# Expert rows that carry their gates, expert outputs stored gated, and early sums behind GpSimd's last store

## The chip, the core and the metric

The kernel runs on one core of a Trainium2 chip: TensorE (PE, with its weight load PEld), VectorE (DVE), ScalarE (ACT), GpSimd (POOL) and SyncE (SP), which work side by side and wait for each other by semaphores, and 16 DMA engines. The metric is device time in microseconds, the median of several runs. All data are float32 (some products are made from a high and a low part).

## The reference, cut to what matters

```
x = x + attn_a(_layernorm(x))      # 8 rows of 512 tokens, 128 wide; 16 heads, softmax
x = x + ffn(_layernorm(x))         # mixture of experts
x = x + attn_b(_layernorm(x))      # linear attention (8 heads) and an MLP
x = x + ffn(_layernorm(x))         # the same mixture of experts again

# ffn, E = 8 experts, K = 2 per token:
probs = softmax(xn @ Wr + br);  scores, idx = top_k(probs, K)
full  = relu(xn @ W1_e + b1_e) @ W2_e + b2_e            # for each expert
c = relu(b1) @ W2 + b2;  c_total = c.sum(axis=0)
output = sum_k scores[k] * (full[idx_k] - c[idx_k] + c_total)
return residual + output
```

So a token's result is a sum of two expert outputs, each plus a constant of its expert and times its gate (the score).

## The kernel before, in words

It runs in three stages: attention (and the first routing), linear attention, MLP (and the second routing). "Row" is one of 8 batch rows of 512 tokens, held as NT = 4 tiles of 128 tokens; with NT tiles per row, x_sb holds the residual.

**Routing** (class Route, `bankR` its PSUM bank). For each row VectorE normalises the tokens into `xn_sb` (profile name f_xn; it is refilled row by row, a ring of 2 or 3), TensorE turns them and makes the logits, ScalarE the exponentials; VectorE takes the two largest (`dve_top`, `dve_topid`), ids and gates (`dve_ids`), and works out in which slot of its expert's region each token's row goes (`dve_place` to `dve_slots`, profile name f_slot). GpSimd then scatters 8 times 128 rows to DRAM (`expert_in`), an indirect DMA each (L703). A row is 130 floats: 128 of the token, the token's number, and the lower one of its two expert ids. `dve_gates` (L679 to L688) puts the two gates in the order of the expert ids into `gates`: six small instructions a row. In the MLP stage the order on VectorE is x_add of the row before, its statistics, two products, then `route_place` with the gates, then the normalisation (L406); on GpSimd a power of the statistics (L367) comes before the eight scatters of the row before, in two halves.

**Experts** (class Experts). Behind each routing, blocks of 256 rows are worked off expert by expert in a loop on all engines. SP loads a block into `xb`; TensorE turns it; VectorE makes `xbT` (L1126); TensorE 8 matmuls up (L1090), ScalarE 4 relus (L1111), TensorE 16 matmuls down (L1100) in two tiles t of 128 tokens. VectorE takes out token number and lower id (`meta`, L1122), works out whether the token's other expert comes first (`second`, L1132) and so the row of `expert_out` to write to (`this_to`, L1137). For each tile it waits until that tile's store of the block before has landed, casts the row numbers (L1143) and adds the expert's constant (L1146, `yb`); GpSimd stores the tile by an indirect DMA (L1158). The order on VectorE within a block: second, this_to, meta and xbT of the next block, cast and y of tile 0, cast and y of tile 1. The first half of `expert_out` has the outputs of each token's lower expert id ("early"), the other half those of its higher one ("late").

**Combine.** SP loads the early rows 0 to 3 (0 and 1 in the first routing) once all experts but the last have stored, the others when the last store has landed. VectorE adds for each tile early output times gate (L758) and late output times gate (L767) to x_sb. In the MLP stage ScalarE's queue then stores each row to the output; in linear attention the rows 2 to 7 are added between other work, two rows ahead.

Of the kernel before, what the change touches and what calls it, by code (L numbers as in the profile page):

```python
# [38 lines left out]
W = D + 2  # L39
# [4 lines left out]
def build_hybrid(nc, x, W_K, W_Q, W_V, W_O, attn_norm_w, Wq, Wk, Wv, Wo, out_norm_w, mlp_norm_w,  # L44
                 Wgate, Wup, Wdown, gamma, beta, Wr, br, W1, b1, W2, b2, out):
    root = ExitStack()
    with root:
# [52 lines left out]
        spare = sb("spare", [1, 16])  # L100
        gates = sb("gates", [P, (B + 1) * NT, TOP])
# [46 lines left out]
        class Startup:  # L148


            CONSTS = 21
            BANKS = (4, 5, 6, 7, 2, 3, 2, 3)

            def __init__(self, at, raw):
# [4 lines left out]
                self.small, self.fill = sem("s_small", at), sem("s_fill", at)  # L159
# [23 lines left out]
            def pool(self, pool):  # L183
                nc.gpsimd.memset(self.zero, 0.0).then_inc(self.fill, 1)
                nc.gpsimd.memset(before_bf[:, :], 0.0).then_inc(self.fill, 1)
                pool.wait_ge(self.fill, 2)
# [23 lines left out]
                nc.gpsimd.memset(gates[:, B * NT:, :], 0.0).then_inc(self.const, 1)  # L210
                nc.gpsimd.memset(fill[:, :, 0:D], 0.0).then_inc(self.const, 1)
                nc.gpsimd.memset(fill[:, :, D + 1], -1.0).then_inc(self.const, 1)
                nc.gpsimd.iota(fill[:, :, D], pattern=[[P, BT]], base=(TOP - 1) * B * T, channel_multiplier=1,
# [276 lines left out]
        class Route:  # L490
# [10 lines left out]
            def __init__(self, name, at, bankR, ring=2, lean=False):  # L501
# [9 lines left out]
                self.topidf = sb(name + "_topidf", [P, NT, E], f32, at=at)  # L511
# [5 lines left out]
                self.gate = sb(name + "_gate", [P, NT, TOP], at=at)  # L517
                self.below = sb(name + "_below", [P, TOP, NT, 1], at=at)
                self.kept_gate = sb(name + "_kept_gate", [P, NT, TOP], at=at)
                self.turned_gate = sb(name + "_turned_gate", [P, NT, TOP], at=at)  # L520
                self.gate_step = sem(name + "_gate_step", at)
# [80 lines left out]
            def dve_ids(self, dve, b, u):  # L602

                self.settle(dve, b, self.TOPID)
                nc.vector.tensor_copy(self.topidf[:, :, :], self.topid[:, :, :]).then_inc(self.step, 1)
                nc.vector.tensor_tensor(self.gate[:, :, :], self.top[:, :, 0:TOP],
                                        self.rrec[:, :, :].to_broadcast([P, NT, TOP]), ALU.mult).then_inc(self.step, 1)

            def dve_is_k(self, dve, b, u):
                self.settle(dve, b, self.IDS)  # L610

                nc.vector.tensor_copy(self.norm.xn_sb[:, u, :, D], token[:, bass.ds(b * NT, NT)]
                                      ).then_inc(self.tagged, 1)
                nc.vector.tensor_tensor(self.norm.xn_sb[:, u, :, D + 1], self.topidf[:, :, 0], self.topidf[:, :, 1],
                                        ALU.min).then_inc(self.tagged, 1)
                for k in range(TOP):
                    nc.vector.tensor_tensor(self.is_k[:, k, :, :],
                                            expert_id[:, :].unsqueeze(1).to_broadcast(self.wide),
                                            self.topidf[:, :, k:k + 1].to_broadcast(self.wide),
# [56 lines left out]
            def dve_gates(self, dve, b, u):  # L676

                first, second = self.topidf[:, :, 0:1], self.topidf[:, :, 1:2]
                nc.vector.tensor_tensor(self.below[:, 0, :, :], first, second, ALU.is_lt).then_inc(self.gate_step, 1)  # L679
                nc.vector.tensor_tensor(self.below[:, 1, :, :], first, second, ALU.is_gt).then_inc(self.gate_step, 1)  # L680
                dve.wait_ge(self.gate_step, 6 * b + 2)
                for k, part in enumerate((self.kept_gate, self.turned_gate)):
                    nc.vector.tensor_tensor(part[:, :, :], self.gate[:, :, :],
                                            self.below[:, k, :, :].to_broadcast([P, NT, TOP]),
                                            ALU.mult).then_inc(self.gate_step, 1)
# [483 lines left out]
        with stage(clear=False) as st:  # L1169
# [69 lines left out]
            with nc.Block(no_gpsimd_drain=True) as block:  # L1239
# [263 lines left out]
                def _(dve):  # L1503
# [121 lines left out]
                    for b in range(2):  # L1625
                        combine.dve_early(dve, b)
# [675 lines left out]
```

## Time and profile before

| | us |
|---|---|
| median of 3 runs (lowest to highest) | 1335.34 (1331.35 to 1336.68) |
| the profiled execution: its own time / its span | 1336.18 / 1333.9 |
| busy PE / DVE / ACT / POOL | 1201.3 / 923.5 / 829.8 / 507.8 |
| POOL's stores of expert outputs, 142 | 139.4 |
| POOL's scatters of tokens, 128 | 126.5 |

The span is the time between the first and the last instruction of the profiled execution. The page cuts it into 40 slices of 33 us; by its rows attention lasts to about 520 us, the first expert blocks from 565 to 697, linear attention from 700 to 1018, the MLP to 1140, its last scatters to 1162, the second expert blocks from 1168 to 1308, and the tail to the end. Busy shares don't say what a change is worth: in each stage another engine has no gap, and an engine's idle time costs only where something else waits for it.

### The profile page before, as it was taken

The numbers are of one execution on the slowest core, as the hardware profiler recorded it, in microseconds if no ns is written. First come the engines' busy times: TensorE is split into PE (matmuls) and PEld (weight loads), VectorE is DVE, ScalarE is ACT, GpSimd is POOL, SyncE is SP. The second block draws the span as 40 slices with busy tenths as digits, with TensorE's granted clock in tenths as the row PEclk, the third lists the DMA queues.
The fourth block names the chain that finished last, engine by engine and source line by source line (L and its number), as shares of the span: only waits on it lengthen the run. The fifth ranks groups of instructions, "written<-read, shape, count | busy, mean of one in ns | idle before, by whom it ended". The sixth has DMA issues, their size and how long they took to land. (4 is left out here: it accounts for less than half of the span.)

```text
span 1333.9 us, 26704 instructions
## 1 busy us (share of the span) xinstructions
PE 1201.3 (90%) x7787; PEld 913.0 (68%) x7787; DVE 923.5 (69%) x3634; ACT 829.8 (62%) x2478; POOL 507.8 (38%) x619
## 2 busy tenths in 40 slices
PE   6999999999999998699975999999996988199991
PEld 4666676666666665499964777777774656189991
DVE  6788888888888875444446888888873676344446
ACT  5898888888989885244432565565555666044440
POOL 2111334142414232545442343443432366635452
PEclk9999999999999999799997999999997999599996
DMA  9100000000000000222222000000000011222226
GB/s 291 53 2 1 12 7 11 7 13 6 17 5 13 7 11 3 77 72 72 69 78 72 9 9 9 9 1 1 1 1 1 13 39 39 74 61 71 70 74 203
DMA packets 54443, 52.90 MB, mean 40 GB/s; under 512 B 7341, under 2 KB 43098, under 8 KB 54330
## 3 DMA queue, kind: packets, MB, share of 16 engines
q1 hardware_dynamic: 36320, 29.39, 7.7%
q0 software_dynamic: 8928, 17.84, 4.0%
q10 hardware_dynamic: 9082, 4.33, 1.1%
q8 instruction: 51, 0.84, 0.3%
q14 instruction: 62, 0.51, 0.1%
HBM read 29.48 MB, written 22.05 MB: 39 GB/s over the span
## 5 line engine op out<-in xcount | busy, mean ns | idle before, releaser
L1462 ACT ACTIVATE prob<-prob,negmax 128x256 f32<-128x256 f32 (+3 forms) x512 | 283.2, 556 | 37.5 <-DVE negmax L1556 37.4
L1556 DVE CUSTOM_DVE_ANT_0 prob<-bank,mask 128x256 f32<-128x256 f32 (+3 forms) x512 | 224.6, 481 | 32.9 <-PE bank L1272 31.2
L1640 POOL TENSOR_TENSOR Vs<-Vh_sb,rinv 128x512 f32<-128x512 f32 x64 | 66.7, 1042 | 355.9 <-DVE rinv L1534 355.9
L1158 POOL DMA_INDIRECT expert_out<-f_x_yb,f_x_to x142 | 139.4, 981 | 155.3 <-DVE f_x_yb L1146 130.8
L1284 PE MATMUL bank<-prob,Vs 128*64 128x512 f32 (+3 forms) x1024 | 153.6, 442 | 2.9 <-POOL Vs L1640 2.8
L703 POOL DMA_INDIRECT expert_in<-f_xn,f_slot x128 | 126.5, 988 | 48.9 <-issue 30.9
L1090 PE MATMUL bank<-f_x_xbT,W_sb 128*128 128x256 f32 x568 | 138.1, 387 | 1.5 <-DVE f_x_xbT L1126 1.5
L1111 ACT ACTIVATE f_x_hid<-bank,cols 128x256 f32<-128x256 f32 x144 | 63.8, 474 | 91.7 <-PE bank L1090 91.7
L1090 PEld LDWEIGHTS bank<-f_x_xbT,W_sb 128*128 128x128 f32 x568 | 104.6, 194 | 14.5 <-DVE f_x_xbT L1126 2.5
L1284 PEld LDWEIGHTS bank<-prob,Vs 128*64 128x64 f32 x1024 | 64.1, 137 | 72.8 <-issue 62.9
L1111 ACT ACTIVATE prob<-bank,cols 128x256 f32<-128x256 f32 x140 | 62.1, 474 | 82.1 <-PE bank L1090 82.1
L1143 DVE CAST f_x_to<-f_x_this_to 128x1 int32<-128x1 f32 x142 | 21.3, 150 | 116.1 <-DMA expert_out<-f_x_yb,f_x_to 115.9
L1462 ACT ACTIVATION_READ_ACCUMULATOR prob<-prob,negmax 128x1 f32 x512 | 97.6, 191 | 0.0
L1851 ACT ACTIVATE yT_hi<-bank 128x512 fp32r<-128x512 f32 x64 | 38.3, 598 | 90.1 <-PE bank L1778 90.1
L1983 DVE SCALAR_TENSOR_TENSOR z_sb<-bank,ro,z_sb 128x128 f32<-128x128 f32 x256 | 88.3, 345 | 6.4 <-POOL ro L1917 2.9
L1272 PE MATMUL bank<-Q_hi,K_hi 64*128 64x256 f32 (+3 forms) x512 | 89.5, 345 | 2.3 <-DVE K_lo L1524 2.3
L1272 PE MATMUL bank<-Q_lo,K_hi 64*128 64x256 f32 (+3 forms) x512 | 83.2, 320 | 0.0
L1272 PE MATMUL bank<-Q_hi,K_lo 64*128 64x256 f32 (+3 forms) x512 | 82.7, 319 | 0.0
L1858 ACT ACTIVATE junk<-bank 128x128 f32<-128x128 f32 x256 | 68.7, 274 | 16.8 <-PE bank L460 4.8
L1272 PEld LDWEIGHTS bank<-Q_hi,K_hi 64*128 64x128 f32 x512 | 48.6, 186 | 42.9 <-issue 39.8
L458 PE MATMUL bank<-WVO_hi,yT_hi 128*128 128x256 f32 x256 | 74.5, 291 | 2.4 <-DVE z_sb L1983 2.4
L460 PE MATMUL bank<-WVO_hi,yT_lo 128*128 128x256 f32 x256 | 72.2, 282 | 0.0
(270 smaller groups left out, 3186.6 us busy)
## 6 DMA issues: line engine op xcount, KB each, us to landing
f_x_xb<-expert_in SPq DMA_DIRECT2D x73, 130.0 KB, 2.2
z_sb<-expert_out SPq DMA_DIRECT2D x20, 256.0 KB, 3.6
expert_out<-f_x_yb,f_x_to POOLq DMA_INDIRECT x142
expert_in<-fill ACTq DMA_DIRECT2D x16, 130.0 KB, 3.0
x_sb<-in_L_attn_a_x_dram SPq DMA_DIRECT2D x8, 256.0 KB, 6.3
W_sb<-in_L_ffn_W_dram SPq DMA_DIRECT2D x1, 2048.0 KB, 9.9
expert_in<-f_xn,f_slot POOLq DMA_INDIRECT x128, 2.4
act_h<-expert_out SPq DMA_DIRECT2D x8, 256.0 KB, 5.7
```

The lines of the kernel that those rows point to most:

```text
L458: nc.tensor.matmul(ps, lhsT_hi, rhs_hi, start=True, stop=False)
L460: return nc.tensor.matmul(ps, lhsT_lo, rhs_hi, start=False, stop=stop)
L703: pool.indirect_dma_start(xg, bass.IndirectOffsetOnAxis(ap=self.slot[:, u, t, k:k + 1], axis=0), self.norm.xn_sb[:, u, t, :], None).then_i ...
L1090: nc.tensor.matmul(self.bankH[c][:, 0:BLK], W1_sb[:, e, c * P:(c + 1) * P], self.xbT[:, :], start=True, stop=True).then_inc(self.up_done[c ...
L1111: nc.scalar.activation(self.hid[:, c, :], self.bankH[c][:, 0:BLK], ACT.Relu, bias=b1_col[:, e * FC + c:e * FC + c + 1]).then_inc(self.hid_ ...
L1158: pool.indirect_dma_start(yg, bass.IndirectOffsetOnAxis(ap=self.to[:, t:t + 1], axis=0), self.yb[:, t, :], None).then_inc(self.stored[t], 16)
L1272: mm = nc.tensor.matmul(score_bank(i, a), left[r, g % 2, tile], right[r, g % 2, 0:width[i]], start=(right is Q_hi and left is K_hi), stop= ...
L1284: mm = nc.tensor.matmul(bankZ[heads, 0:width[i]], Vs[:, g % 2, i, heads], prob[:, g % 2, a, columns(i)], start=(i == 3), stop=(i == 2), sk ...
L1462: nc.scalar.activation(mine, mine, ACT.Exp, scale=-1.0, bias=negmax[:, g % 2, i, a:a + 1], accum_out=rowsum[:, g % 2, i, a:a + 1]).then_in ...
L1556: nc.vector.tensor_tensor_reduce(out=prob[:, g % 2, a, columns(i)], in0=score_bank(i, a), in1=mask[:, T - width[i]:], scale=-1.0, scalar=H ...
L1858: ins = nc.scalar.activation(junk[:, s % 2, m, :], bankO[s % 2 * 2 + m // 2][:, m % 2 * (DB + D):m % 2 * (DB + D) + DB], ACT.Square, accum ...
L1983: nc.vector.scalar_tensor_tensor(out=tile, in0=bankO[s % 2 * 2 + m // 2][:, o:o + D], scalar=ro[:, s % 2, m:m + 1], in1=tile, op0=ALU.mult ...
```

## The change

1. A scattered row grows from 130 to 134 floats: token, two gates, token number, lower id, two ids. The cast of ids and the multiplication that makes the gates write straight into `xn_sb`. `dve_gates`, `gates` and their six instructions a row are gone.
2. In the expert loop VectorE copies the six tags of a row and works out for each token the gate of this expert and the row to write to: three instructions into `part` and `meta`, and one sum `gate_to`. ScalarE multiplies the expert's constant by the gate, two activations a block behind the relus (`gated_const`). y is now PSUM times gate plus `gated_const`, one scalar_tensor_tensor a tile.
3. The sums of Combine are plain: one tensor_tensor of 128x512 for each row in place of four scalar_tensor_tensor.
4. GpSimd does a small memset behind its last store is issued (`all_issued`), and VectorE waits for it before the first early sums, in both routings.

```diff
-W = D + 2
+GATE, TOKEN, LOW_ID, IDS = D, D + TOP, D + TOP + 1, D + TOP + 2
+W = IDS + TOP
@@ Route
-                nc.vector.tensor_copy(self.topidf[:, :, :], self.topid[:, :, :]).then_inc(self.step, 1)
-                nc.vector.tensor_tensor(self.gate[:, :, :], self.top[:, :, 0:TOP],
+                tags = self.norm.xn_sb[:, u, :, :]
+                nc.vector.tensor_copy(tags[:, :, IDS:IDS + TOP], self.topid[:, :, 0:TOP]).then_inc(self.step, 1)
+                nc.vector.tensor_tensor(tags[:, :, GATE:GATE + TOP], self.top[:, :, 0:TOP],
                                         self.rrec[:, :, :].to_broadcast([P, NT, TOP]), ALU.mult).then_inc(self.step, 1)
-            def dve_gates(self, dve, b, u):
...
@@ Combine
-                for t in range(NT):
-                    tile = x_sb[:, b * NT + t, :]
-                    nc.vector.scalar_tensor_tensor(
-                        out=tile, in0=self.early[:, b * NT + t, :], scalar=gates[:, b * NT + t, 0:1],
-                        in1=tile, op0=ALU.mult, op1=ALU.add).then_inc(self.early_added, 1)
+                row = x_sb[:, b * NT:(b + 1) * NT, :]
+                nc.vector.tensor_tensor(row, row, self.early[:, b * NT:(b + 1) * NT, :],
+                                        ALU.add).then_inc(self.early_added, 1)
@@ Experts.act_work
+                    act.wait_ge(self.gate_to_ready, k + 1)
+                    for t in range(BT):
+                        act.wait_ge(self.y_ready[t], k)
+                        ins = nc.scalar.activation(self.gated_const[:, t, :], moe_const[:, e, :], ACT.Copy,
+                                                   scale=self.gate_to[:, t, 0:1])
+                    ins.then_inc(self.const_ready, 1)
@@ Experts.dve_work
-                    nc.vector.tensor_copy(self.meta[:, :, :], self.xb[:, :, D:D + 2]).then_inc(self.meta_ready, 1)
+                    nc.vector.tensor_copy(self.meta[:, :, :], self.xb[:, :, D:]).then_inc(self.meta_ready, 1)
...
+                    gate, low_id, first_id = self.meta[:, :, 0:TOP], self.meta[:, :, LOW_ID - D], self.meta[:, :, IDS - D]
+                    nc.vector.tensor_scalar(self.part[:, :, 1], low_id, float(e), float(B * T),
+                                            ALU.not_equal, ALU.mult)
+                    nc.vector.scalar_tensor_tensor(out=self.part[:, :, 0], in0=first_id, scalar=float(e),
+                                                   in1=gate[:, :, 0], op0=ALU.is_equal,
+                                                   op1=ALU.mult)
+                    nc.vector.scalar_tensor_tensor(out=gate[:, :, 1], in0=first_id, scalar=float(e),
+                                                   in1=gate[:, :, 1], op0=ALU.not_equal,
+                                                   op1=ALU.mult).then_inc(self.parts_known, 1)
...
+                        if t == 0:
+                            dve.wait_ge(self.const_ready, k + 1)
                         dve.wait_ge(self.down_done[t], k + 1)
-                        nc.vector.tensor_tensor(self.yb[:, t, :], self.bankY[t][:, 0:D],
-                                                moe_const[:, e, :], ALU.add).then_inc(self.y_ready[t], 1)
+                        nc.vector.scalar_tensor_tensor(
+                            out=self.yb[:, t, :], in0=self.bankY[t][:, 0:D], scalar=self.gate_to[:, t, 0:1],
+                            in1=self.gated_const[:, t, :], op0=ALU.mult, op1=ALU.add).then_inc(self.y_ready[t], 1)
@@ Experts.pool_work, behind the loop
+                nc.gpsimd.memset(spare[:, 16:17], 0.0).then_inc(self.all_issued, 1)
@@ both routings
                     experts.dve_work(dve, counts)
+                    dve.wait_ge(experts.all_issued, 1)
```

On VectorE in the MLP stage, before, between the slots of one row and the normalised tokens of the next:

```order
L666 TENSOR_REDUCE f_slotf<-f_picked 128x8
L674 CAST f_slot<-f_slotf 128x8
L679 TENSOR_TENSOR f_below<-f_topidf 128x4
L680 TENSOR_TENSOR f_below<-f_topidf 128x4
L683 TENSOR_TENSOR f_kept_gate<-f_gate,f_below 128x8
L683 TENSOR_TENSOR f_turned_gate<-f_gate,f_below 128x8
L688 TENSOR_TENSOR gates<-f_kept_gate,f_turned_gate 128x4 x2
L406 TENSOR_SCALAR f_xn<-x_sb,f_mv,f_power 128x128 x4
```

and at the same place now:

```order
L655 CAST run_bf<-f_run 128x8
L659 TENSOR_REDUCE f_slotf<-f_picked 128x8
L667 CAST f_slot<-f_slotf 128x8
L405 TENSOR_SCALAR f_xn<-x_sb,f_mv,f_power 128x128 x4
L373 TENSOR_SCALAR f_power<-f_power 128x4
```

The six instructions of the gates are gone, and f_xn follows f_slot.

On VectorE in the last expert's blocks, a turn of the loop before:

```order
L1132 TENSOR_SCALAR f_x_second<-f_x_meta 128x2
L1137 TENSOR_TENSOR f_x_this_to<-f_x_second,f_x_meta 128x2
L1120 REGISTER_ALU
L1122 COPY f_x_meta<-f_x_xb 128x4
L1125 REGISTER_ALU
L1126 TENSOR_SCALAR f_x_xbT<-bank,cols 128x256
L1142 REGISTER_ALU
L1143 CAST f_x_to<-f_x_this_to 128x1
L1146 TENSOR_TENSOR f_x_yb<-bank,moe_const 128x128
L1143 CAST f_x_to<-f_x_this_to 128x1
L1146 TENSOR_TENSOR f_x_yb<-bank,moe_const 128x128
```

and now:

```order
L1116 TENSOR_SCALAR f_x_part<-f_x_meta 128x2
L1118 SCALAR_TENSOR_TENSOR f_x_part<-f_x_meta 128x2
L1121 SCALAR_TENSOR_TENSOR f_x_meta<-f_x_meta 128x2
L1127 TENSOR_TENSOR f_x_gate_to<-f_x_part,f_x_meta 128x4
L1103 REGISTER_ALU
L1105 COPY f_x_meta<-f_x_xb 128x12
L1108 REGISTER_ALU
L1109 TENSOR_SCALAR f_x_xbT<-bank,cols 128x256
L1132 REGISTER_ALU
L1133 CAST f_x_to<-f_x_gate_to 128x1
L1138 SCALAR_TENSOR_TENSOR f_x_yb<-bank,f_x_gate_to,f_x_gated_const 128x128
```

Two more small instructions stand ahead of meta and xbT, and y has another form; the rest of the turn is in the same order.

## Rows read from the trace of the kernel before

**Rows 1.** The page's 40 slices, TensorE's busy tenths.

```profile
PE   6999999999999998699975999999996988199991
```

**Rows 2.** Order in time, VectorE, MLP stage: start us, busy us, instruction, [idle before <-releaser].

```profile
1111.60 0.17 DVE L674 CAST f_slot<-f_slotf 128x8 int32<-128x8 f32 x1
...
1112.38 1.31 DVE L406 TENSOR_SCALAR f_xn<-x_sb,f_mv,f_power 128x128 f32<-128x128 f32 x4
```

**Rows 3.** Order in time, MLP stage, ScalarE and TensorE, one row earlier.

```profile
1095.49 1.26 ACT L2133 ACTIVATE m_xn<-z_sb,mlp_rstd 128x128 f32<-128x128 f32 x4
...
1099.48 0.66 PE L431 MATMUL bank<-ident,f_xn 128*128 128x128 f32 x4 [1.30 <-DVE f_xn L406]
```

**Rows 4.** Order in time, GpSimd, MLP stage.

```profile
1109.85 1.67 POOL L367 TENSOR_TENSOR f_power<-f_power,half 128x8 f32<-128x8 f32 x1
1112.63 1.03 POOL L703 DMA_INDIRECT expert_in<-f_xn,f_slot  x1 [1.11 <-DVE f_slot L674]
...
1124.20 1.67 POOL L367 TENSOR_TENSOR f_power<-f_power,half 128x8 f32<-128x8 f32 x1
...
1140.11 1.67 POOL L367 TENSOR_TENSOR f_power<-f_power,half 128x8 f32<-128x8 f32 x1 [2.12 <-DVE f_power L362]
```

**Rows 5.** Order in time, second expert stage, all engines, one turn of the loop.

```profile
1204.95 1.89 PE L1090 MATMUL bank<-f_x_xbT,W_sb 128*128 128x256 f32 x8
...
1205.58 1.77 ACT L1111 ACTIVATE f_x_hid<-bank,cols 128x256 f32<-128x256 f32 x4 [1.97 <-PE bank L1090]
1206.29 0.15 DVE L1143 CAST f_x_to<-f_x_this_to 128x1 int32<-128x1 f32 x1 [1.75 <-DMA expert_out<-f_x_yb,f_x_to]
1206.36 0.28 DVE L1146 TENSOR_TENSOR f_x_yb<-bank,moe_const 128x128 f32<-128x128 f32 x1
...
1207.43 0.54 DVE L1126 TENSOR_SCALAR f_x_xbT<-bank,cols 128x256 f32<-128x256 f32 x1
1207.46 0.96 POOL L1158 DMA_INDIRECT expert_out<-f_x_yb,f_x_to  x1 [1.14 <-DVE f_x_yb L1146]
1207.54 0.37 SPq L1049 DMA_DIRECT2D f_x_xb<-expert_in  x1
...
1207.99 0.29 DVE L1146 TENSOR_TENSOR f_x_yb<-bank,moe_const 128x128 f32<-128x128 f32 x1
...
1208.68 1.89 PE L1090 MATMUL bank<-f_x_xbT,W_sb 128*128 128x256 f32 x8
...
1209.94 0.15 DVE L1143 CAST f_x_to<-f_x_this_to 128x1 int32<-128x1 f32 x1 [1.66 <-DMA expert_out<-f_x_yb,f_x_to]
```

**Rows 6.** Waits of VectorE, second expert stage: us in total, times, longest.

```profile
DVE f_x_to L1143 <- DMA expert_out<-f_x_yb,f_x_to: 57.9, 37, 2.4
```

**Rows 7.** Order in time, VectorE and GpSimd, the tail.

```profile
1308.18 4.28 DVE L758 SCALAR_TENSOR_TENSOR x_sb<-z_sb,gates,x_sb 128x128 f32<-128x128 f32 x16
1308.83 1.06 POOL L1158 DMA_INDIRECT expert_out<-f_x_yb,f_x_to  x1 [2.46 <-DVE f_x_yb L1146]
1310.19 3.11 POOL L1158 DMA_INDIRECT expert_out<-f_x_yb,f_x_to  x1 [0.30 <-issue]
...
1317.36 4.29 DVE L758 SCALAR_TENSOR_TENSOR x_sb<-z_sb,gates,x_sb 128x128 f32<-128x128 f32 x16 [4.90 <-DMA z_sb<-expert_out]
1321.57 8.49 DVE L767 SCALAR_TENSOR_TENSOR x_sb<-act_h,gates,x_sb 128x128 f32<-128x128 f32 x32
```

**Rows 8.** Busy time by stretch: second expert stage, tail (PEclk, DMA share, GB/s last).

```profile
1169.00:1307.00 138.00, 136.70 (x936) 126.43 (x936) 61.92 (x285) 63.82 (x144) 67.20 (x70) 0.99 0.26 76
...
1316.00:1332.50 16.50, 0.00 (x0) 0.00 (x0) 12.70 (x48) 0.00 (x0) 0.00 (x0) 0.50 0.97 314
```

**Rows 9.** The page's costliest groups: xcount | busy us, mean ns | idle before.

```profile
L1983 DVE SCALAR_TENSOR_TENSOR z_sb<-bank,ro,z_sb 128x128 f32<-128x128 f32 x256 | 88.3, 345 | 6.4 <-POOL ro L1917 2.9
```

**Rows 10.** Groups of instructions, VectorE, MLP stage.

```profile
L2185 DVE TENSOR_TENSOR x_sb<-x_sb,bank 128x512 f32<-128x512 f32 x8 | 5.4, 678 | 3.9 <-PE bank L2095 3.9
```

**Rows 11.** Order in time, VectorE, end of the first expert stage.

```profile
700.94 1.14 DVE L767 SCALAR_TENSOR_TENSOR x_sb<-x_sb,gates 128x128 f32<-128x128 f32 x4 [3.71 <-DMA x_sb<-expert_out]
```

More of the change, by code:

```diff
@@ L98, in build_hybrid @@
         mlp_rstd = sb("mlp_rstd", [P, B * NT])
-        spare = sb("spare", [1, 16])
-        gates = sb("gates", [P, (B + 1) * NT, TOP])
+        spare = sb("spare", [1, 17])
         token = sb("token", [P, (B + 1) * NT])
@@ L674, in dve_slots @@
                 nc.vector.tensor_copy(self.slot[:, u, :, :], by_tile).then_inc(self.slot_ready, 1)
-            def dve_gates(self, dve, b, u):
[L678 to L685, printed above, removed]
-                dve.wait_ge(self.gate_step, 6 * b + 4)
-                for k in range(TOP):
-                    nc.vector.tensor_tensor(gates[:, b * NT:(b + 1) * NT, k], self.kept_gate[:, :, k],
-                                            self.turned_gate[:, :, 1 - k], ALU.add).then_inc(self.gate_step, 1)
             def dve_normalise(self, dve, b, u):
@@ L735, in load_late @@
                 if b >= self.ring:
[L736 removed]
+                    sp.wait_ge(self.late_added, b + 1 - self.ring)
                 sp.dma_start(self.late[b % self.ring],
@@ L755, in dve_early @@
                 self.early_landed(dve, b)
-                for t in range(NT):
-                    tile = x_sb[:, b * NT + t, :]
-                    nc.vector.scalar_tensor_tensor(
-                        out=tile, in0=self.early[:, b * NT + t, :], scalar=gates[:, b * NT + t, 0:1],
-                        in1=tile, op0=ALU.mult, op1=ALU.add).then_inc(self.early_added, 1)
+                row = x_sb[:, b * NT:(b + 1) * NT, :]
+                nc.vector.tensor_tensor(row, row, self.early[:, b * NT:(b + 1) * NT, :],
+                                        ALU.add).then_inc(self.early_added, 1)
             def dve_late(self, dve, b):
                 self.late_landed(dve, b)
-                dve.wait_ge(self.early_added, (b + 1) * NT)
-                for t in range(NT):
-                    tile = x_sb[:, b * NT + t, :]
-                    nc.vector.scalar_tensor_tensor(
-                        out=tile, in0=self.late[b % self.ring][:, t, :], scalar=gates[:, b * NT + t, 1:2],
-                        in1=tile, op0=ALU.mult, op1=ALU.add).then_inc(self.late_added, 1)
+                dve.wait_ge(self.early_added, b + 1)
+                row = x_sb[:, b * NT:(b + 1) * NT, :]
+                nc.vector.tensor_tensor(row, row, self.late[b % self.ring], ALU.add).then_inc(self.late_added, 1)
             def row_added(self, eng, b):
-                eng.wait_ge(self.late_added, (b + 1) * NT)
+                eng.wait_ge(self.late_added, b + 1)
             def dve_complete(self, dve, b):
```

78 lines of the change are left out of this document (34 added, 44 removed).

## Prediction, made before the changed kernel ran

> **What bounds the kernel now.** I first read the page's slices: from 33 to 500 us (attention) and from 734 to 1000 (linear attention) TensorE has nines only [rows 1]. What VectorE is spared there is worth next to nothing. In each of the other stretches I then looked in the order of time for the engine that never idles. Three places are left.
>
> The MLP stage (1020 to 1160) goes round a ring. VectorE normalises a row only behind six tiny instructions that work out the gates: f_slot starts at 1111.60, f_xn at 1112.38 [rows 2]. TensorE stands idle for that f_xn, 1.30 us in the row before [rows 3]. GpSimd is the ring's other half: its power starts at 1109.85, then it waits 1.11 for f_slot and issues eight scatters up to the next power at 1124.20 [rows 4].
>
> The expert stages are two loops with nearly one period. TensorE's up matmuls start at 1204.95 and 1208.68, 3.73 us a block. The other is the store loop of a block's second tile: the cast of its row numbers at 1206.29, y at 1206.36, GpSimd's store at 1207.46, and the next cast at 1209.94, held until that store landed: 3.65 [rows 5]. In the second expert stage 37 such waits add up to 57.9 us [rows 6], so practically every block has one. The page's 142 stores are 71 blocks in both stages together.
>
> The tail: 16 early sums start at 1308.18; GpSimd's second-to-last store takes 1.06 and its last one 3.11; the first row loaded afterwards is summed at 1317.36, and from 1321.57 VectorE adds late rows for 8.49 us [rows 7], while the DMA engines are 97% busy from 1316 to 1332.5 [rows 8].
>
> **The change part by part.** All sums are made against the profiled execution: span 1333.9 us, 1336.18 with what lies around it, 0.84 above the median of the runs, 1335.34.
>
> *Gates of a row, removed in both routings.* In attention they stand beside a TensorE that is full: zero. In the MLP stage the six lie between f_slot and f_xn: 1112.38 - 1111.60, less one step of 0.08, is 0.70 us a row [rows 2]. They stand ahead of f_xn in six rows and once ahead of the last x_add. f_xn also needs GpSimd's power, though. That ended at 1109.85 + 1.67 = 1111.52 [rows 4], as good as tied with f_slot, so the first row affected gains some 0.65 and no more. The power of the row after comes a fixed way behind this f_slot: 1111.77 (its end), 0.86 to the first scatter, 11.57 to the power, 1.67 of power, 1125.87. A row can therefore gain 0.65 over the row two before it: 0.6, 0.7, 1.25, 1.3, 1.9, 1.95. The seventh gates lie in front of the last x_add, and there GpSimd waits 2.12 for VectorE at 1140.11 [rows 4], so the whole 0.70 is had. Behind it GpSimd scatters without a gap, and that shifts as a whole. **-2.6 us**; bounds 0 (GpSimd takes all of it) and 7 x 0.70 = -4.9.
>
> *Tags in the scattered rows.* Ids and gates go into f_xn by the cast and the multiply that were there. Rows grow from 520 to 536 bytes, 3%. Zero; bounds 0 and 3% of a store's 2.48 to landing, 0.07 a block, which is part of rival A.
>
> *Expert loop, VectorE.* y becomes a scalar_tensor_tensor of PSUM, a scalar and an SBUF operand. That form takes 345 ns in linear attention [rows 9], y now 280 [rows 5]: +0.06. The loop was 0.07 + 0.28 + 0.82 + 2.48 = 3.65 and becomes 3.71, where its landings are longer up to 3.76. Two more small instructions delay xbT by 2 x 0.07 and y's 0.06, 0.2 in all. xbT ends at 1207.43 + 0.54 = 1207.97, its up matmul starts at 1208.68 [rows 5]: 0.7 of cover becomes 0.5. Were it gone, each further tenth would cost 7 us.
>
> *Expert loop, ScalarE.* Two copies of 128x128 with a scale follow the four relus, which end at 1205.58 + 1.77 = 1207.35 [rows 5]. Four such copies take 1.26 in the MLP stage [rows 3], two about 0.65: 1208.0. y of the first tile started at 1207.99, so it may come 0.1 late. Nothing waits for that tile's store, since VectorE is held by the second tile's until 1209.94. Zero in the period, 0.1 at the end of each stage; bound 0.1 in each block, 7 us, if the first tile's store became the later one.
>
> *What the loop costs.* Each block's second cast waits for a landing, so y's 0.061 comes through in each: 68 of them, **+4.1 us**. Bounds: 0, if TensorE's 3.73 is the only limit and 3.71 stays under it. Upwards: the block's load is issued at 1207.54, 0.08 behind the store [rows 5]; it moves by 0.2, the store by 0.06. If this 0.14 and the bigger rows all come onto the landing, 71 x 0.2 = 14 more.
>
> *Stores gated, sums plain.* One tensor_tensor of 128x512 takes the place of four instructions. The nearest row is x_add with as many columns, 0.68 [rows 10]; now a row takes 8.49 / 8 = 1.06. At the end of the first expert stage the late sum of row 0 takes 1.14 from 700.94, with nothing beside it [rows 11]: **-0.5**. In linear attention 12 such sums save 5 us of VectorE under a full TensorE: 0, bound -0.5.
>
> *The wait for GpSimd's last store.* In the last tail the store was stretched from about 1 us to 3.11 beside the early sums. With VectorE silent it should take 1.06: -2.05. Behind the wait stand four early sums, 4 x 0.65 = 2.6, from about 1311.5 to 1314.1, and the next row's data comes no earlier than 1317.36 - 2.05 = 1315.3: covered. In the first expert stage two sums wait and are done near 699, before 700.94: covered. Twelve sums then take 7.8 where they took 12.7, but the DMA engines are full: 12 loads and 8 stores of 256 KB at 314 GB/s are 16.5 us [rows 8]. Bounds 0 and -4.9; I take -1.2, near zero, because stores can only begin earlier among the loads. **-3.3** for the tail.
>
> The Trainium skill, SBUF — State Buffer, "Who interferes with whom", speaks against this term: a VectorE instruction with two SBUF inputs contends with a GpSimd instruction that reads SBUF, not with one that only writes there. If an indirect store is mostly writing of descriptors, the early sums never held it, and the tail gains 1.2 rather than 3.3. The trace has both answers, 1.06 for one store and 3.11 for the next beside the same sums [rows 7].
>
> I go by 3.11, since the sums end at 1308.18 + 4.28 = 1312.46 and the store only 0.84 after them, nearly a whole store's time.
>
> Sum: -2.6 - 0.5 - 3.3 + 4.1 = -2.3. From 1336.18 that is 1333.9, and at the median **1333.0 us**.
>
> **The rivals.**
> A, slower: the landing of the second tile's store grows, by the mechanism above: the block's load, issued later against it, shares more of its time. Price 0.14 a block, 71 x 0.14 = 10: 1343.0. It makes the kernel slower than before from 2.3 / 71 = 0.03 a block, and measurably from 9 / 71 = 0.13. For it: the loop waits for nothing else; against: both transfers fall into one window already.
> B, faster: TensorE's period stays the limit (+1), GpSimd follows so that the MLP stage gains 4.5, and the tail gains 4.5 with the 0.5 before linear attention: -8.5, 1326.8. For it: TensorE is busy 136.70 of 138 us [rows 8]. Against: rows 6, and the power tied with f_slot.
> C, the wait frees nothing: the 3.11 came from something else, so the change doesn't do here what it says. For it: the neighbour's 1.06. Tail -1.2: 1335.1. The rule of the Trainium skill named above would have it so.
>
> **How the numbers follow.** Forecast 0.45, A 0.15, B 0.23, C 0.17. Under about 0.5%, 6.7 us, a measurement of this kernel can't tell from no change: faster means under 1328.7, slower over 1342.0. Faster: most of B and a little of the forecast, 0.23. Slower: two thirds of A and the forecast's upper edge, 0.12. Same: 0.65. The range runs from 1326 (0.09 below) to 1342 (0.11 above).
>
> **What would show it.** f_xn directly behind f_slot or behind power, and the way from row to row 0.3 shorter. y at 345 ns, the second cast still waiting for DMA in every block, a loop of 3.71 to 3.76, an expert stage some 2 us longer. The last store at about 1 us, and late sums with gaps that wait for DMA. The forecast is wrong if the up matmuls stay at 3.73 throughout (B), if store to cast takes over 2.6 in most blocks (A), or if the last store still takes 3 us (C).

## The result and the profile after

The changed kernel takes 1338.84 us (median of 20 runs, 1335.97 to 1344.25) where the kernel before took 1334.67 beside it (20 runs, 1330.77 to 1337.47). The ratio is 1.0036, 95% interval 1.0025 to 1.0047: 4.8 us slower (3.3 to 6.3), where I had forecast 2.3 less. That is under the half per cent which I took as the bound of what a time can tell; with 20 runs of each kernel it stands clear of the noise all the same.

The profiled executions differ by 5.2 us (spans 1333.89 and 1339.04). Cut at events that both programs have (GpSimd's first and last store of each expert stage, its second power, L367 before and L366 after, of the MLP stage), the difference splits up like this; the last column is the same cut through a second profile of the kernel before (experiment 12):

```
stretch                              before    after    difference   before, again
start to first store of stage 1      564.6     561.5    -3.1         562.4
expert stage 1, first to last store  131.3     139.2    +7.9         132.2
last store to power in MLP           356.7     355.5    -1.1         355.5
power to first store of stage 2      123.0     120.2    -2.8         122.9
expert stage 2, first to last store  134.6     141.3    +6.7         135.2
last store to the end                 23.7      21.3    -2.4          22.5
span                                1333.9    1339.0    +5.2        1330.7
```

The loss lies in the two expert stages, 14.6 us; every other stretch became shorter. One turn of the loop in the second of them, VectorE, in order of time (start us, busy us, instruction, [idle before <- releaser]):

```profile
1220.44 0.15 DVE L1133 CAST f_x_to<-f_x_gate_to 128x1 int32<-128x1 f32 x1 [1.73 <-DMA expert_out<-f_x_yb,f_x_to]
1220.51 0.34 DVE L1138 SCALAR_TENSOR_TENSOR f_x_yb<-bank,f_x_gate_to,f_x_gated_const 128x128 f32<-128x128 f32 x1
1220.85 0.17 DVE L1116 TENSOR_SCALAR f_x_part<-f_x_meta 128x2 f32<-128x2 f32 x1
...
1221.19 0.17 DVE L1127 TENSOR_TENSOR f_x_gate_to<-f_x_part,f_x_meta 128x4 f32<-128x4 f32 x1
1221.46 0.17 DVE L1105 COPY f_x_meta<-f_x_xb 128x12 f32<-128x12 f32 x1
1221.75 0.54 DVE L1109 TENSOR_SCALAR f_x_xbT<-bank,cols 128x256 f32<-128x256 f32 x1
...
1224.29 0.15 DVE L1133 CAST f_x_to<-f_x_gate_to 128x1 int32<-128x1 f32 x1 [1.68 <-DMA expert_out<-f_x_yb,f_x_to]
```

Against [rows 5]: the turn is 3.85 instead of 3.65. y is 0.06 longer, as forecast; the store starts at 1221.67 and the next cast comes 2.62 later, where it was 2.48. Over the whole stretch from 1180 to 1300, the time from one block's first up matmul to the next one's went from 3.73 to 3.94 in the mean, and the time from the second tile's store to the cast that waits for it from 2.52 to 2.71 in the median. So 0.2 of the landing stands beside y's 0.06, not 0 to 0.05. In the kernel before, every single block of that stretch took TensorE 3.73 or 3.74: TensorE never waited, and it was the limit. Now it no longer runs through, as it did in [rows 8]; it waits for the block's load, and xbT ends only at 1222.29, just before its up matmul, so that no cover is left (TensorE and its weight loads, same turn):

```profile
1220.29 0.20 PEld L1061 LDWEIGHTS bank<-ident,f_x_xb 128*128 128x128 f32 x2 [0.25 <-DMA f_x_xb<-expert_in]
1220.29 0.44 PE L1061 MATMUL bank<-ident,f_x_xb 128*128 128x128 f32 x2
1222.35 0.48 PE L1067 MATMUL bank<-f_x_xbT,W_sb 128*128 128x256 f32 x1
```

VectorE's waits in the second expert stage (us in total, times, longest) still have a landing in nearly every block, as [rows 6] had:

```profile
DVE f_x_to L1133 <- DMA expert_out<-f_x_yb,f_x_to: 61.5, 39, 2.6
```

The MLP stage gained about as much as was forecast (how much of that is luck, see below). f_xn follows f_slot at once where GpSimd's power is not the later one; in other rows power now is the later one (VectorE, against [rows 2]):

```profile
1101.29 0.17 DVE L667 CAST f_slot<-f_slotf 128x8 int32<-128x8 f32 x1
1102.13 1.28 DVE L405 TENSOR_SCALAR f_xn<-x_sb,f_mv,f_power 128x128 f32<-128x128 f32 x4 [0.67 <-POOL f_power L366]
...
1115.48 0.17 DVE L667 CAST f_slot<-f_slotf 128x8 int32<-128x8 f32 x1
1115.62 1.11 DVE L405 TENSOR_SCALAR f_xn<-x_sb,f_mv,f_power 128x128 f32<-128x128 f32 x4
```

The tail, GpSimd and VectorE, against [rows 7]: the last store takes 0.96, early sums 0.62 each, late sums with one gap that waits for DMA.

```profile
1317.77 0.96 POOL L1151 DMA_INDIRECT expert_out<-f_x_yb,f_x_to  x1 [0.30 <-issue]
1318.73 0.09 POOL L1155 MEMSET spare<- 1x1 f32 x1
1318.85 2.50 DVE L735 TENSOR_TENSOR x_sb<-x_sb,z_sb 128x512 f32<-128x512 f32 x4 [2.55 <-POOL spare L1155]
1322.78 1.34 DVE L735 TENSOR_TENSOR x_sb<-x_sb,z_sb 128x512 f32<-128x512 f32 x2 [1.43 <-DMA z_sb<-expert_out]
...
1328.29 4.04 DVE L742 TENSOR_TENSOR x_sb<-x_sb,act_h 128x512 f32<-128x512 f32 x6 [0.57 <-DMA act_h<-expert_out]
```

Last, the late sum at the end of the first expert stage, 0.45 shorter than in [rows 11]:

```profile
705.72 0.69 DVE L742 TENSOR_TENSOR x_sb<-x_sb 128x512 f32<-128x512 f32 x1 [2.62 <-DMA x_sb<-expert_out]
```

### The profile page after: what moved, and what is told of

Same layout as the page of the kernel before. It is cut to its first block and busy times, and to the rows that moved or that the text cites. A ratio compares the mean times of both kernels' runs of the same rounds, so it can differ in the third digit from the quotient of the medians.

```text
span 1339.0 us, 26945 instructions
## 1 busy us (share of the span) xinstructions
PE 1214.7 (91%) x7787; PEld 914.2 (68%) x7787; DVE 916.5 (68%) x3584; ACT 878.0 (66%) x2620; POOL 504.9 (38%) x620
## 5 line engine op out<-in xcount | busy, mean ns | idle before, releaser
L1067 PE MATMUL bank<-f_x_xbT,W_sb 128*128 128x256 f32 x568 | 143.4, 396 | 2.1 <-DVE f_x_xbT L1109 1.8
L1133 DVE CAST f_x_to<-f_x_gate_to 128x1 int32<-128x1 f32 x142 | 21.2, 149 | 123.8 <-DMA expert_out<-f_x_yb,f_x_to 123.8
L458 PE MATMUL bank<-WVO_lo,yT_hi 128*128 128x256 f32 x256 | 72.9, 285 | 0.0
```

The costliest lines, as they stand in the source:

```text
L458: nc.tensor.matmul(ps, lhsT_hi, rhs_lo, start=False, stop=False)
L1067: nc.tensor.matmul(self.bankH[c][:, 0:BLK], W1_sb[:, e, c * P:(c + 1) * P], self.xbT[:, :], start=True, stop=True).then_inc(self.up_done[c ...
```

## The experiments

Every ratio is to the kernel before, run beside it on the same chip, with 5 to 12 executions of each kernel but the twelfth; the 95% interval stands in brackets, and 0.001 is 1.3 us. "Period" is the mean time from a block's first up matmul on TensorE to the next block's, from 1180 to 1300 of the profile. "Landing" is the median time from the start of the second tile's store to the cast that waits for it, from 1180 to 1295. In the kernel before they are 3.73 and 2.52, in the changed one 3.94 and 2.71. Of the edits only the lines that matter are shown; cuts are marked "...".

**1. Longer rows alone.**

```diff
-W = D + 2
+W = D + 6
 ...
```

> The kernel before with only its scattered rows made longer, 134 elements in place of 130 (536 bytes in place of 520); the four added elements carry copies of the lower id, no instruction is added, and the gates stay where they were. It asks why the two expert stages of the changed kernel are 14.6 us longer (131.3 to 139.2 and 134.6 to 141.3). Theory 1, the block load of 256 longer rows runs beside the second tile's store and holds it up: the store's landing grows from 2.54 to about 2.7 us and the kernel takes +8 to +14 us, 1343 to 1349. Theory 2, the row's size doesn't count and the landing grows because VectorE issues the load later or writes y more slowly: 1334.7, within 1 us of the kernel before.

Ratio 1.0024 (1.0009 to 1.0039), period 3.73, landing 2.55. The period is no longer than before and the landing 0.03 longer, not 0.2. By its times the size costs some 3 us (1.2 to 5.2), which lies outside both expectations and which its own profile, with stages of 132.6 and 135.0 us, doesn't place. Theory 1 fell as the main cause.

**2. Two small VectorE instructions ahead of the tags' copy.**

```diff
+for m in range(2):
+    nc.vector.scalar_tensor_tensor(out=self.more[:, :, m], in0=self.meta[:, :, 1], scalar=float(e), ...)
 nc.vector.tensor_scalar(self.second[:, :], self.meta[:, :, 1], ...)
```

> The kernel before with two more small VectorE instructions (0.15 us in all) ahead of those that make a block's row numbers, so that the copy of the tags, and with it the issue of the next block's load and the normalisation of the next block, come later behind the second tile's y, as in the changed kernel. Theory 1, phase of the load: the load then overlaps the store's 128 row writes longer, the landing grows by 0.14 to 0.2 and the kernel takes +8 to +14 us. Theory 2, the chain behind y has slack (the normalised block is there 0.6 to 0.7 us before TensorE wants it): within 1 us of the kernel before, 1334.7.

Ratio 1.0081 (1.0060 to 1.0103): 10.8 us from 0.15 us a block. Period 3.93, landing 2.77: the changed kernel's loss with the old y, the old rows and no gates in them. TensorE's weight loads wait for the block's load 25 times, 6.6 us in all from 1180 to 1295, as in the changed kernel (25 times, 6.5), and not once in the same stretch of the kernel before's first profile.

**3. y's form alone.**

```diff
-nc.vector.tensor_tensor(self.yb[:, t, :], self.bankY[t][:, 0:D], moe_const[:, e, :], ALU.add)
+nc.vector.scalar_tensor_tensor(out=self.yb[:, t, :], in0=self.bankY[t][:, 0:D], scalar=unit[:, 0:1],
+                               in1=moe_const[:, e, :], op0=ALU.mult, op1=ALU.add)
```

> The kernel before with y written as SCALAR_TENSOR_TENSOR (bank times a column of ones, plus the constant) in place of TENSOR_TENSOR, 0.34 in place of 0.28 us, and nothing else. My forecast: the 0.06 stands in the loop of the second tile's stores, so +4.1 us over 71 blocks, 1338.8. Rival: TensorE's own period of 3.73 us a block is the limit before, and VectorE's loop has up to 0.06 us of slack under it (3.65 us between two casts that follow each other in the middle of the stage): +0 to +1 us, about 1335. The changed kernel's loop would then be longer by its landing alone.

Ratio 1.0007 (0.9993 to 1.0022), 0.9 us; y 0.34, period 3.75, landing 2.50. My 4.1 stands outside the interval, which ends at 2.9. Most of the 0.06 fell into slack under TensorE's 3.73.

**4. The changed kernel without ScalarE's constants.** It leaves out the product of constant and gate, so its output is another one; y adds the constant as it is.

```diff
-    ins = nc.scalar.activation(self.gated_const[:, t, :], moe_const[:, e, :], ACT.Copy, scale=self.gate_to[:, t, 0:1])
-if t == 0:
-    dve.wait_ge(self.const_ready, k + 1)
 ...
```

> The changed kernel without ScalarE's gated constants: y adds the ungated constant (so the constant's gating is left out of the computation), and VectorE no longer waits for ScalarE ahead of the first tile's y. Theory 1, the constants cost nothing, as forecast, since ScalarE has 1 us to spare a block: within 1 us of the changed kernel, 1338.8. Theory 2, the first tile's y waits for them or their SBUF traffic slows VectorE: the expert stages are 0.1 us a block shorter, 1331 to 1333.

Ratio 1.0028 (1.0018 to 1.0038), against 1.0036 (1.0025 to 1.0047) of the changed kernel; period 3.92, landing 2.72. The constants cost nothing that stands clear of the noise.

**5. The wait for the last store alone.**

```diff
+nc.gpsimd.memset(spare[:, 16:17], 0.0).then_inc(self.all_issued, 1)
 ...
+dve.wait_ge(experts.all_issued, 1)
```

> The kernel before with only the wait: VectorE's gated sums start when GpSimd's small fill behind its last store instruction has run, in both expert stages. Expected by the tail of the changed kernel (from the start of the last store 23.7 us before, 21.2 after): the last store instruction 0.96 to 1.1 us instead of 3.11, and 1.5 to 2.5 us less, 1332.5 to 1333. Rival: the sums that no longer run beside the store come at the end, where they are as late, and nothing is gained: 1334.7 to 1336.

Ratio 0.9995 (0.9985 to 1.0004). The last store takes 0.96, but only 0.7 us come of it (at most 2.0), less than I expected. Experiment 12 says why.

**6 and 7. Gates of all rows put in order once behind each expert loop; in 7 with the wait as well.**

```diff
-if b < LAST:
-    route.dve_gates(dve, b, slot_of(b))
 ...
 experts.dve_work(dve, counts)
+route.dve_gates(dve)          # five instructions of 128x32 for all rows
 ...
```

> The kernel before with the gates of all rows put in order once, by five VectorE instructions behind the last block of each expert stage, in place of six per row inside the attention and MLP stages; rows, expert loop and sums as before. Expected if the gates stood on VectorE's path: the MLP stage 2.5 to 3 us shorter as in the changed kernel, and the attention stage up to 3 us shorter if its 3.1 us also came from there; 1329 to 1332. Rival: the 3.1 us of the attention stage came from elsewhere (startup, clock): 1332 to 1333. Against both: the five instructions stand ahead of the first sums, at most +1 us at the end.

> The gates of all rows put in order once behind the expert loop, and the wait for the last store as well: the changed kernel's gains without its expert loop. If gains add: 1327 to 1330. If the tail's gain is used up by the five instructions that make the gates: 1331 to 1332.

Both 0.9966 (0.9954 to 0.9979), 4.5 us faster. The stretch from power to the first store is 119.4 and 119.3 us, in eight profiles with the gates inside 122.5 to 123.3: -3.5. The first stretch is 562.1 and 562.5, as in the second profile of the kernel before (562.4), so attention gained nothing. The wait added nothing either.

**8. The changed kernel with its load earlier.** The tags are copied out between the two y's, so that from there on only the transposes hold the next load.

```diff
+                        if t == 0:
+                            raw(k + 2, k16 + 32)      # copy of xb's tags, releases the load
-nc.vector.tensor_copy(self.meta[:, :, :], self.xb[:, :, D:]).then_inc(self.meta_ready, 1)
+nc.vector.tensor_copy(self.meta[:, :, :], self.raw[:, :, :])
 ...
```

> The changed kernel with one more copy a block: the tags are copied out of the loaded block between the two tiles' y, ahead of the wait for the second store, and from there to the place where they were copied before, so that the next load is issued by the transposes (about 0.7 to 1 us earlier) and no longer by the second tile's y. Theory phase: now load and second store move in one burst of about 1.0 us, where a store alone takes 0.3 to 0.4; apart, the landing falls from 2.7 to 2.2 to 2.4 us and the loop from 3.93 to TensorE's 3.73, 10 to 14 us less: 1325 to 1329. Rival: the landing hangs on the longer chain behind y and not on the load: 1338 to 1340, landing still 2.7.

Ratio 0.9974 (0.9961 to 0.9988), 8.3 us less than the changed kernel. The expert stages went from 139.2 and 141.3 to 132.7 and 137.0 us; the median period is 3.73, the mean 3.78, and y now waits for TensorE. The load did not come earlier in every block by the 0.7 to 1 us that I had expected. In 19 of the 30 blocks from 1180 to 1295 it is issued within 0.25 us of the second store's start, and the landing's median there is 2.47; in the ten in which it comes 0.4 to 1.4 us ahead, the landing is 2.24 or 2.25. So the load may be well ahead of the store as well as well behind it. The time missed its range by 2 us: the period stayed 0.05 above TensorE's, and the MLP stretch, 122.2 here, kept little of its gain.

**9. Two small instructions behind the tags' copy**: a pair of the same form as in the second experiment (on constants), between `meta_ready` and `xbT`.

> The kernel before with the same two small VectorE instructions as in the second experiment (0.15 us in all), but behind the copy of the tags: the next block's load is issued as early as before, and only the normalised block and the first tile's y come 0.15 us later. Theory phase of the load: nothing moves, landing 2.54 to 2.57, within 1 us of the kernel before, 1335. Rival, the later normalised block is what lengthens the loop: landing 2.7, the kernel as slow as with the two instructions ahead of the copy, 1343 to 1346.

Ratio 0.9991 (0.9975 to 1.0006), period 3.75, landing 2.55. The same 0.15 us, put behind the load's release, costs nothing that shows (at most 0.8 us).

**10. The load later in the kernel before.**

```diff
 sp.wait_ge(self.meta_ready, k)
+sp.wait_ge(self.xbT_ready, k)
```

> The kernel before with the next block's load held until the normalised block is written, 0.5 to 0.6 us later than now, and nothing else. If each 0.1 us by which the load comes later lengthens the store's landing by about as much, as it did from 0 to 0.15 us: the loop 4.1 us or more, 1350 to 1362. If the store's rows are then moved ahead of the load's: landing 2.2 to 2.4, TensorE's 3.73 the limit and 1333 to 1336, as long as the load lands before the transposes (a slack of about 0.4 us now).

Ratio 0.9969 (0.9955 to 0.9984): 4.1 us faster, which lies below both expected ranges. Landing 2.26, median period 3.73, as the second expectation had them. The expert stages are 264.2 us together, against 265.9 and 267.4 in the two profiles of the kernel before; that places 1.7 to 3.2 of the 4.1 us.

**11. The changed kernel without its wait for the last store** (the two lines of experiment 5 taken out).

> The changed kernel without VectorE's wait for GpSimd's last store: the plain sums start behind the last y. If the sums hold the last store up as the gated ones did in the profile before: last store 3 to 3.5 us, the first loads for the sums about 2 us later, and 1 to 2 us more than the changed kernel (1340 to 1341). Rival: it is an accident of single executions (of six profiles without the wait so far, three show 3.1 us and two 1.0): within 0.7 us of the changed kernel.

Ratio 1.0014 (1.0001 to 1.0028). Last store 0.95 beside plain sums, nothing gained by waiting. The kernel is if anything faster than the changed one, by 0.0022 or 2.9 us, where either ratio is uncertain by 0.0011 to 0.0014; neither expectation had that.

**12. The kernel before, a second look.**

> The kernel before once more, for a second profile. It tells which parts of the difference between the two profiles are mere scatter between executions: I expect the first pair of the attention stage at 6.85 or 8.2 to 9.2 us behind the first, the attention stage 471.6 to 473.3 us from its third pair to its last, the last store 1.0 or 3.1 us; and the loop's period 3.73 to 3.76 and the MLP stage 122.7 to 123.3 us as in every profile with its code.

Span 1330.7 in a single execution, 3.2 less than in the first profile: 2.3 less in the first stretch, 1.1 before the MLP stage and 1.2 in the tail, against 1.4 more in the expert stages. MLP stretch 122.9, period 3.74, landing 2.54. And beside the same 16 gated sums the last store takes 1.06, not 3.11 (GpSimd and VectorE):

```profile
1307.30 4.28 DVE L758 SCALAR_TENSOR_TENSOR x_sb<-z_sb,gates,x_sb 128x128 f32<-128x128 f32 x16
1308.20 1.06 POOL L1158 DMA_INDIRECT expert_out<-f_x_yb,f_x_to  x1 [0.53 <-issue]
```

Of eleven profiles of kernels without the wait (the one of before, experiments 1 to 3, 6, 9 to 12, 14, 15) three have a last store of 3.1 us, one of 1.5 and seven of about 1.0. The four long ones start 1.8 to 2.0 us into the run of sums and end 0.83 or 0.84 us behind that run (experiment 15, whose run of four plain sums is shorter, has the 1.5). The seven short ones start at most 1.5 us into it. So what varies is where in the run of sums the last store falls; in the first profile it fell 2.01 us in, here 0.90.

**13. The changed kernel with its load later.** The one added line of experiment 10.

> The changed kernel with the next block's load held until the normalised block is written (0.5 to 0.6 us later), and nothing else. Theory, the whole loss of the expert stages is the load's transfer inside the second store's: landing 2.2 to 2.3 in place of 2.7, the loop back to TensorE's 3.73, expert stages 11 to 14 us shorter, 1325 to 1328. Rival, the longer chain behind y limits as well, since the load must now land before the transposes, which already wait 0.25 us for it in the changed kernel: loop 3.85 to 3.95, 1335 to 1339.

Ratio 0.9945 (0.9930 to 0.9960), median 1326.42: 7.3 us faster than the kernel before and 12.1 faster than the changed one (0.9945 against 1.0036). Landing 2.25, median period 3.73, expert stages 130.1 and 135.4, together 15.0 us less. The whole loss is won back, and this version beats both kernels. TensorE's up matmuls and VectorE's second tile, one turn apart:

```profile
1213.60 1.89 PE L1068 MATMUL bank<-f_x_xbT,W_sb 128*128 128x256 f32 x8
1217.34 1.89 PE L1068 MATMUL bank<-f_x_xbT,W_sb 128*128 128x256 f32 x8
```

```profile
1213.94 0.15 DVE L1134 CAST f_x_to<-f_x_gate_to 128x1 int32<-128x1 f32 x1 [0.60 <-DMA expert_out<-f_x_yb,f_x_to]
...
1217.68 0.15 DVE L1134 CAST f_x_to<-f_x_gate_to 128x1 int32<-128x1 f32 x1 [0.60 <-DMA expert_out<-f_x_yb,f_x_to]
```

**14 and 15. Both gains in the kernel before; the thirteenth without the wait.**

> The kernel before with the gates put in order once behind each expert loop (sixth experiment, 0.9966) and the load held until the normalised block is written (tenth, 0.9969). They lie in different stages and should add: 0.9935, 1325 to 1327. If not, 1330.

> The thirteenth kernel (changed kernel, load late) without VectorE's wait for GpSimd's last store. If the wait saves the 2 us of a held-up store: this one 1 to 2 us slower than the thirteenth. If the store is held up in few executions and the wait only pushes the sums back: the same or up to 2 us faster, as the eleventh was against the changed kernel.

Fourteen: 0.9959 (0.9945 to 0.9972), so the two gains seem to add in part only; its interval ends just above the 0.9935 expected. Fifteen: 0.9946 (0.9933 to 0.9960), the same as thirteen. The wait is worth nothing that shows here, though this profile's last store is a held one (1.50).

## What the load and the store do to each other

The DMA engines' busy share in 40 slices of 0.1 us, with the rate in GB/s under it, show how the two transfers meet. First the kernel before, 1210 to 1214 us: its second store starts at 1211.11, its load is issued at 1211.23.

```profile
DMA  0000009710000000000000855889985000000000
GB/s 0 0 0 0 0 0 369 246 41 0 0 0 0 0 0 0 0 0 0 0 0 0 42 94 135 182 250 378 418 299 190 0 0 0 0 0 0 0 0 0
```

The first tile's store moves in some 0.25 us; load and second store share one burst from 1212.2 to 1213.1. The changed kernel, 1221 to 1225, second store at 1221.67:

```profile
DMA  8910000000000000003675799971000000000008
GB/s 287 328 41 0 0 0 0 0 0 0 0 0 0 0 0 0 0 0 21 96 107 96 241 309 352 464 289 52 0 0 0 0 0 0 0 0 0 0 0 287
```

The burst ends at 1223.8, 2.1 behind the store's start where it was 2.0 in the kernel before, and the cast follows 0.5 later in both. The kernel of experiment 10, 1213.05 to 1217.05, stores at 1214.13 and 1215.39:

```profile
DMA  0990000024589963100000000097000000000069
GB/s 0 328 328 0 0 0 0 0 26 99 146 208 255 260 182 109 42 5 0 0 0 0 0 0 0 0 410 246 0 0 0 0 0 0 0 0 0 0 246 328
```

The bursts stand apart: each store moves by itself in 0.2 us, 1.5 behind its instruction's start, and the load lies between them. The same in the kernel of experiment 13, from 1213.10:

```profile
DMA  0960000379599640000000000293000000000078
GB/s 0 410 246 0 0 0 0 38 102 155 166 263 284 204 140 22 0 0 0 0 0 0 0 0 0 82 451 123 0 0 0 0 0 0 0 0 0 0 287 287
```

The DMA packets in the traces tell the two transfers apart. Medians over the blocks from 1180 to 1295, in us from the start of the second tile's store:

| kernel | load issued | load's packets | store's packets | cast (landing) |
|---|---|---|---|---|
| before | 0.12 | 1.13 to 1.99 | 1.63 to 2.15 | 2.52 |
| experiment 9 | 0.15 | 1.14 to 2.01 | 1.62 to 2.18 | 2.55 |
| changed | 0.20 | 1.21 to 2.17 | 1.70 to 2.33 | 2.71 |
| experiment 2 | 0.26 | 1.27 to 2.21 | 1.75 to 2.37 | 2.77 |
| experiment 13 | 1.12 | 2.13 to 2.98 | 1.53 to 1.87 | 2.25 |
| experiment 10 | 1.26 | 2.25 to 3.11 | 1.53 to 1.88 | 2.26 |

In every one of them the cast follows 0.38 us, give or take 0.01, behind the store's last packet. Where the two meet, the store's last packet ends 0.15 to 0.17 behind the load's last one: the store is done when the load is. So a later load makes a later landing. Of the 0.19 that the changed kernel's landing grew, 0.08 is the later issue and most of the rest a transfer of 0.95 us where it was 0.86; in experiment 2 it is 0.14 and 0.93. Why the load's own transfer takes longer there, no run tells. TensorE's wait for the load has no part in it: the load is released by the copy of the tags (1221.46 in the turn above), 0.7 behind the end of the transposes.

The Trainium skill, DMA: Bandwidth & Descriptors, "Queues, rings and completion order", has each DMA engine take turns between the queues that have work, a whole packet from one before it turns to the next. The shared burst, with the packets of both queues mixed in time, agrees with that as far as it goes; the traces don't say which engine moved which packet.

## Why the prediction failed, by its steps

*Expert loop, y.* The term +4.1 was wrong, and so was its reason that each block's landing wait passes y's 0.06 on. Alone it costs 0.9 us (at most 2.9). A landing wait in every block isn't proof that the loop of stores sets the period: TensorE was busy 136.70 of 138 us in [rows 8], and its 3.73 was the limit. Rival B had that right for the kernel before.

*Expert loop, the load's issue.* This is the step that failed. I wrote the shift down (load later by 0.14 against the store), named it rival A with 10 us, and left it out of the sum because "both transfers fall into one window already". They did, and that was the reason for it, not against it: inside a shared burst the store's last packet ends with the load's. The shift was smaller than written down, 0.08 in the median and not 0.14, but the landing grew by 0.19, more than rival A's 0.14. The two expert stages grew by 14.6 us. The shift of experiment 2 alone costs 10.8 us, and experiment 13 takes 15.0 away from the stages with one wait. The loop's upper bound, +4.1 + 14, held it. The sign I had given for rival A, store to cast over 2.6 in most blocks, is what the profile shows.

*Cover of xbT.* Put at 0.7 to 0.5 us with 7 us for each tenth once gone. It was gone in the changed kernel (up matmul 1222.35, xbT ended 1222.29), yet experiment 9, which delays xbT by the same 0.15, costs nothing, and in experiment 13, with the changed kernel's instructions, it is back. So its loss came with the longer period and did not cause it.

*ScalarE's constants.* Nothing in the period, as forecast (experiment 4).

*Tags in the rows.* Put at zero, at most 0.07 a block; times give 3.2 us (1.2 to 5.2), which would be 0.02 to 0.07 a block. That is within the bound but not zero; no profile places it in the blocks.

*Gates out of the MLP stage.* Forecast -2.6, measured -2.8, and -3.5 in experiment 6; the mechanism is right, f_xn behind f_slot or behind power as described. That the number fits is partly luck. The forecast's gain had to lie ahead of the stage's last power; from the second power to there the changed kernel gained 1.7 us (87.5 to 85.8), and the other 1.1 lies behind it, where I had nothing. Five more profiles have the same routing: in three (experiments 4, 11, 13) the whole stretch is 3.5 to 3.7 us shorter than before, in two (8 and 15, 122.2) only 0.7. Why they differ stays open.

*Sums.* The late sum of the first stage gave 0.45 of the 0.5 forecast. From the last store to the MLP stage six profiles with plain sums have 353.6 to 355.5 us, eleven with gated ones 355.1 to 357.4, so linear attention gives another 1 us or so where I had nothing. In the tail plain sums leave 20.8 to 21.7 us behind the last store's start, gated ones 21.7 to 22.5 where that store isn't held up: some -0.8 of the -1.2.

*The wait.* The -2.05 was taken from one profile. The store is held up only where it falls late in the run of sums (four of eleven profiles), so the wait's worth is a share of it: 0.7 us by experiment 5, nothing between 13 and 15, and in the changed kernel the wait seems to cost rather than gain (experiment 11). The profiled tails differ by 2.4 us, but only because the first profile's last store was a held one; against tails whose store isn't, the gain is 0.8. Rival C, with -1.2 for the tail, was nearer than my -3.3. The rule of the Trainium skill behind it, SBUF — State Buffer, "Who interferes with whom", that a VectorE instruction with two SBUF inputs contends with a GpSimd instruction that reads SBUF and not with one that only writes it, is neither borne out nor refuted: the store took 3.11 beside such sums in one execution and 1.06 beside the same sums in another, and no run shows what it reads.

*Not forecast at all* were the 3.1 us of the first stretch. They are most likely scatter: the kernel before has 564.6 and 562.4 in two profiles, and the code that the changed kernel and experiment 4 share up to there has 561.5 and 566.3.

In place of -2.6 - 0.5 - 3.3 + 4.1 = -2.3 the two profiles have -2.8 - 1.1 - 2.4 + 14.6 = +8.3, less the 3.1 of the first stretch, +5.2; the times say +4.8. The range, 1326 to 1342, held the time, but that is no merit of the forecast: the change went the other way, and a loss of 14.6 us was partly hidden by gains elsewhere.

## What to carry to other kernels

Where a load and an indirect store are issued within 0.3 us of each other and the loop waits for the store, look at the DMA engines' busy slices, and at which transfer ends last, before pricing instructions: here 0.15 us of added work ahead of the load's release cost 10.8 us, the same work behind it nothing, and one more wait on the load gained 4 us in the kernel before and 12 in the changed one. Take no term from a single profile's outlier; a second profile of the same kernel showed that both the 3.11 us store and 2 us of the first stretch come and go. And if two loops have nearly the same period (3.65 and 3.73 here), price a change against both.

## What the runs showed of the hardware

A store of 128 rows of 512 bytes by GpSimd's indirect instruction moves its bytes in 0.2 to 0.25 us when alone, 1.5 us behind the instruction's start, and lands at 2.25; beside a load of 130 KB it lands at 2.5 to 2.8, its last packet 0.15 to 0.17 us behind the load's. Waiting longer before issuing the load made the loop faster. The last store's instruction, 0.96 us as a rule, took 3.10 or 3.11 in three executions, each time until 0.8 us after VectorE's run of sums had ended; the kernel of experiment 3:

```profile
1312.14 4.28 DVE L758 SCALAR_TENSOR_TENSOR x_sb<-z_sb,gates,x_sb 128x128 f32<-128x128 f32 x16
1312.73 1.12 POOL L1159 DMA_INDIRECT expert_out<-f_x_yb,f_x_to  x1 [2.30 <-DVE f_x_yb L1146]
1314.15 3.10 POOL L1159 DMA_INDIRECT expert_out<-f_x_yb,f_x_to  x1 [0.30 <-issue]
```

Counting the 1.50 us of experiment 15, it happened in the four executions in which the store began 1.8 us or more after the sums did, and in none of the seven in which it began at most 1.5 us after them. The store before it, 0.6 us into the same sums here, took 1.12. Why a store that begins late is held until the end of the run, no run tells.
